# Local attention with the masks cleared on POOL, and zero products at several places of a 16-layer kernel

## The reference

```python
# L3 b: local attention, 16 heads of 8 features, window 128
rel = k_off[None, :] - bs - q_off[:, None]        # bs = 128, keys of three blocks
mask = (abs(rel) <= 128) & valid
scores = where(mask, (q @ k.T) / sqrt(8), -inf)
out = softmax(scores) @ v;  x = x + out @ Wo.T + bo
# L1 a: causal attention with ALiBi slopes, 16 heads of 8 features
# L1 b: LSH attention with 8 hashes
# L2 a: RWKV-6: token shift, five mixtures of x by a narrow product, tanh and
#       a product per kind, then the projections w, r, k, v, g, then a scan
```

## Time and profile before

| | |
|---|---|
| time, three runs | 3257.56 us (median; 3245.51 to 3259.83) |
| the profiled execution | 3265.36 us, span of its records 3263.6 us |
| busy in it | PE 2808.0 us (86%), DVE 1848.9, ACT 1364.3, POOL 766.0 |
| mean granted clock | 0.927 |
| local attention, main stage | from 2946.3 us, the last turned strip's exponentials at 3156.9 |
| RWKV projections, PE's list | from 2258.5 us to 2335 |

### The profile page before, as it was taken

How to read it: one execution, slowest core, us unless ns; L and a number is a source line. 1 busy time by engine, 2 the same in 40 slices (tenths; PEclk the granted TensorE clock), 3 DMA queues, 4 the chain that set the end, 5 groups by cost and what they waited for, 6 DMA issues and landing times. The chain is left out here.

```text
span 3263.6 us, 54321 instructions
## 1 busy us (share of the span) xinstructions
PE 2808.0 (86%) x21112; PEld 1409.7 (43%) x21112; DVE 1848.9 (57%) x3584; ACT 1364.3 (42%) x2665; POOL 766.0 (23%) x725
## 2 busy tenths in 40 slices
PE   6667788999988888899678888898888899888988
PEld 3454375333466333344322222343233444665546
DVE  4424553798762688401588888302495554636744
ACT  3314244533243376632367677422303233234552
POOL 1000063365254200000653240001460001240003
PEclk9788699999999799999779999998899999998999
DMA  3031011222012311000212010000340001022102
GB/s 120 16 102 46 14 43 48 61 70 70 8 49 81 83 26 32 2 1 0 62 30 34 17 19 2 1 1 12 85 134 1 1 1 52 15 78 55 33 13 78
DMA packets 84391, 130.01 MB, mean 40 GB/s; under 512 B 15585, under 2 KB 52929, under 8 KB 82857
## 3 DMA queue, kind: packets, MB, share of 16 engines
q1 hardware_dynamic: 71528, 106.68, 12.0%
q0 software_dynamic: 9152, 16.71, 2.1%
q10 hardware_dynamic: 3456, 3.15, 0.3%
HBM read 99.93 MB, written 25.85 MB: 39 GB/s over the span
## 5 line engine op out<-in xcount | busy, mean ns | idle before, releaser
L1839 DVE TENSOR_REDUCE at_mp<-PS 128x1 f32<-128x384 f32 (+3 forms) x640 | 306.6, 536 | 84.6 <-PE PS L1660 72.4
L1788 ACT ACTIVATE at_pt<-PS 128x384 f32<-128x384 f32 (+3 forms) x704 | 270.3, 455 | 190.0 <-PE PS L1660 156.9
L1652 PE MATMUL PS<-at_kx,at_qx 48*128 48x384 bf16 (+5 forms) x640 | 198.7, 347 | 39.7 <-DVE at_mp L1839 19.8
L113 PE MATMUL PS<-zeros 128*128 128x512 bf16 x834 | 204.0, 389 | 1.2 <-DVE mx_y L1010 1.2
L1680 PE MATMUL PS<-at_qx,at_kx 57*128 57x512 bf16 (+5 forms) x704 | 192.7, 314 | 9.8 <-ACT at_pt L1788 9.4
L4510 DVE CUSTOM_DVE_ANT_0 PS<-PS,ls_pt 128x1024 f32<-128x1024 f32 x128 | 153.9, 1239 | 20.9 <-ACT ls_pt L4363 12.4
L4363 ACT ACTIVATE ls_pt<-PS,ls_far 128x512 f32<-128x512 f32 x256 | 155.3, 686 | 20.9 <-PE PS L4184 16.9
L1660 PE MATMUL PS<-at_above,identb 64*128 64x128 bf16 (+1 forms) x1408 | 161.2, 212 | 0.0
L1660 PE MATMUL PS<-at_other,at_eye 64*128 64x128 bf16 (+1 forms) x1408 | 158.7, 208 | 0.0
L2568 DVE TENSOR_TENSOR_SCAN mb_ring<-PS,mb_ring 128x1024 f32<-128x1024 f32 x64 | 146.6, 2291 | 18.1 <-POOL mb_ring L2501 6.8
L1161 DVE SCALAR_TENSOR_TENSOR X<-PS,small_L,X 128x512 f32<-128x512 f32 x8 | 6.0, 751 | 261.1 <-PE PS L1108 261.1
(11 more groups left out here) (839 smaller groups left out, 6321.7 us busy)
## 6 DMA issues: line engine op xcount, KB each, us to landing
rw_arena<-rw_v_rows SPq DMA_DIRECT2D x32, 512.0 KB, 4.7
dl_arena<-in_fir_bank SPq DMA_DIRECT2D x32, 256.0 KB, 3.2
lnA<-mb_rows SPq DMA_DIRECT2D x16, 512.0 KB, 3.6
XN<-mb_rows SPq DMA_DIRECT2D x16, 512.0 KB, 3.7
ffn_place<-in_ffn_L SPq DMA_DIRECT2D x4, 1152.0 KB, 17.2
x_rows<-mx_t SPq DMA_DIRECT2D x16, 256.0 KB, 2.7
mx_s<-y_rows SPq DMA_DIRECT2D x16, 256.0 KB, 5.0
ffn_place<-in_ffn_L SPq DMA_DIRECT2D x4, 1024.0 KB, 8.1
```

What stands on the lines that cost most here:

```text
L113: k.nc.tensor.matmul(k.PS[:, bank, :], k.zeros16[:, 0:P], k.zeros16[:, :], start=start, stop=start, skip_group_check=True)
L1652: mm = nc.tensor.matmul(PS[:, n % 3, 0:e - c], QX[rows, u % 3, g, blk(i, P)], KX[rows, u % 3, g, c:e], start=True, stop=True)
L1788: nc.scalar.activation(PT[:, y % SLOTS, g, 0:e - c], PS[:, 3 + n % 3, 0:e - c], ACT.Exp, scale=SCALE).then_inc(exp_done, 1)
L1839: nc.vector.tensor_reduce(best, sc, AX.X, ALU.max).then_inc(s_maxed, 1)
```

## The change

In the local attention the turned scores get no masks any more. `cleared` is a new semaphore: once the four exponentials of a strip are there, POOL sets those in the masked triangles to zero (one `affine_select` for each block of `cuts`, over four heads), and the values wait for POOL instead of ACT. `SLOTS` is 4 instead of 3, and the values of a strip are issued two steps after its turned scores instead of one (`LAG`). Ahead of the values of each strip but the first of a half stand two zero products into bank 6; ahead of the maxima of the second half stand four into bank 7. In both attentions `free_misc` comes ahead of the wait for `padded`, three zero products stand in each of the four last steps of the tail, in place of three at the end, and the projections end with 60 instead of 44 (local) and 88 instead of 68 (causal). RWKV: `linger` 12 instead of 6, 14 zero products ahead of the third `narrow`, 3 ahead of the third product of each `mix`. LSH: `linger` 30 instead of 6.

```diff
-    SLOTS = 3
+    SLOTS, LAG = (3, 1) if causal else (4, 2)
...
-                    keep_pe_busy(k, 2, 68 if causal else 44)
+                    keep_pe_busy(k, 2, 88 if causal else 60)
...
-                    if not cuts[x]:
+                    if not (causal and cuts[x]):
                         mm.then_inc(st_ready, 1)
...
                 def values(u, x):
                     h, j, c, e = second[x]
-                    pe.wait_ge(exp_done, N2 * u + HG * x + HG)
+                    if not causal and x != opens[h]:
+                        keep_pe_busy(k, 6, 2, start=False)
+                    if causal:
+                        pe.wait_ge(exp_done, N2 * u + HG * x + HG)
+                    else:
+                        pe.wait_ge(cleared, G2 * u + x + 1)
...
                 def turn_maxima(u, h):
+                    free_misc("m")
+                    if h and not causal:
+                        keep_pe_busy(k, MISC, 4)
                     pe.wait_ge(padded, 2 * u + h + 1)
-                    free_misc("m")
...
+                        if p == UNITS + 1 and x >= 8:
+                            pe.wait_ge(s_maxed, N1 * UNITS)
+                            keep_pe_busy(k, 0, 3)
...
-                        if 1 <= p <= UNITS and 1 <= x <= G2:
-                            values(p - 1, x - 1)
+                        if 1 <= p <= UNITS and LAG <= x < G2 + LAG:
+                            values(p - 1, x - LAG)
...
-                pe.wait_ge(s_maxed, N1 * UNITS)
-                keep_pe_busy(k, 0, 3)
...
-                        if 1 <= p <= UNITS and x == closes[0] + 1:
+                        if 1 <= p <= UNITS and x == closes[0] + LAG:
                             take_output(p - 1, 0)
...
+                def clear(u, x):
+                    h, j, c, e = second[x]
+                    pool.wait_ge(exp_done, N2 * u + HG * x + HG)
+                    for i in cuts[x]:
+                        sign = 1 if i <= j else -1
+                        part = PT[:, (G2 * u + x) % SLOTS, :, i * P - c:(i + 1) * P - c]
+                        ins = pool.affine_select(out=part, in_=part, compare_op=ALU.is_ge, fill=0.0, base=0, pattern=[[0, HG], [sign, P]], channel_multiplier=-sign)
+                    ins.then_inc(cleared, 1)
...
-        layernorm(k, k.X, k.XN, beside=layer_constants)
+        layernorm(k, k.X, k.XN, beside=layer_constants, linger=12)
...
                 def narrow(b):
+                    if b == 2:
+                        keep_pe_busy(k, 6, 14)
...
+                        if i == 2:
+                            if b >= 3:
+                                pe.wait_ge(e_done, b - 2)
+                            keep_pe_busy(k, 6, 3)
...
-            layernorm(k, k.X, k.XN, beside=layer_constants)
+            layernorm(k, k.X, k.XN, beside=layer_constants, linger=30)
```

More of the change, by code:

```diff
@@ L1618, in head_attention @@
         OT, ON, OC = sb("at_ot", [P, 2, BLK]), sb("at_on", [P, BATCH, NT, P]), sb("at_oc", [P, 2, BLK])
-        with stage(nc, "s_ready", "s_maxed", "padded", "m_turned", "own_d", "m_split", "st_ready", "exp_done", "pv_done",
+        with stage(nc, "s_ready", "s_maxed", "padded", "m_turned", "own_d", "m_split", "st_ready", "exp_done", "cleared", "pv_done",
                    "ot_done", "o_turned", "rec_done", "normed", "gathered", "oc_done", "y_ready", "y_added") as (
-                block, s_ready, s_maxed, padded, m_turned, own_d, m_split, st_ready, exp_done, pv_done,
+                block, s_ready, s_maxed, padded, m_turned, own_d, m_split, st_ready, exp_done, cleared, pv_done,
                 ot_done, o_turned, rec_done, normed, gathered, oc_done, y_ready, y_added):
@@ L1686, in turned_masks @@
                     h, j, c, e = second[x]
-                    for i in cuts[x]:
-                        mm = mask(3 + n % 3, i * P - c, 1 if i <= j else 0, head_second(t) // EACH)
-                    if cuts[x]:
+                    if causal and cuts[x]:
+                        for i in cuts[x]:
+                            mm = mask(3 + n % 3, i * P - c, 1, head_second(t) // EACH)
                         mm.then_inc(st_ready, 1)
@@ L1794, in _, with slopes @@
                         take_output(p - 1, 1)
-            if causal:
-                @block.gpsimd
-                def _(pool):
+            @block.gpsimd
+            def _(pool):
+                def slopes():
                     for u in range(1, UNITS):
@@ L1802, in _ @@
                         load_slopes(pool, u)
+                def clear(u, x):
+                    h, j, c, e = second[x]
+                    pool.wait_ge(exp_done, N2 * u + HG * x + HG)
+                    for i in cuts[x]:
+                        sign = 1 if i <= j else -1
+                        part = PT[:, (G2 * u + x) % SLOTS, :, i * P - c:(i + 1) * P - c]
+                        ins = pool.affine_select(out=part, in_=part, compare_op=ALU.is_ge, fill=0.0, base=0, pattern=[[0, HG], [sign, P]], channel_multiplier=-sign)
+                    ins.then_inc(cleared, 1)
+                if causal:
+                    slopes()
+                else:
+                    for u in range(UNITS):
+                        for x in range(G2):
+                            clear(u, x)
             @block.sync
```

## The result

The changed kernel takes 3277.21 us (median of 19 runs, 3261.61 to 3291.29), the kernel before 3259.56 (19 runs, 3245.51 to 3281.86). The ratio is 1.0044, with a 95% interval of 1.0028 to 1.0059: 14.3 us slower (9 to 19; the two medians lie 17.7 apart), less than the 0.5% that the prediction took as its bound. Forecast were 3269 us, a range of 3241 to 3293, and "same" as the likeliest class. The profiled execution took 3278.16 us with a span of 3276.4.

What follows compares the result with a forecast made beforehand. PE was taken to bound the local attention loop, as a chain of score, exponential, fourth score and values at full clock. Loop +30 and repairs -18.5 gave +11.5 us: 3269 us by the median, 3276.9 as profiled; range 3241 to 3293.

Steps and rivals of the forecast that it cites:

- The local loop: Local attention's eight units: added zeros and later values outweigh the removed masks, +3.8 us a unit, +30 us in all.
- the pairs: Two zero products ahead of 8 of 10 products with values: 0.54 us each, 4.3 us a unit, 0.4 hidden.
- the four: Four zero products ahead of the second half's maxima in the local attention: 1.0 us a unit.
- the masks: 112 turned mask products taken off PE in each local attention unit, only partly on the path: -2.3 us a unit.
- The delay: Local attention values two steps later: PE stands 0.8 us for the output copy, about 0.4 at a unit's head.
- The repairs: Added zeros and lingers outside the loop's steps raise the clock: -18.5 us in all, bounds -6 and -30.
- RWKV: RWKV projections: zeros lift the clock, mostly behind the third narrow product; -11 us, bounds -5 and -18.5.
- LSH: Start of the LSH layer: 24 more zeros fill a wait of 6.60 us; -2.5 us, bounds 0 and -3.6.
- The first unit: First unit of the local attention: 16 more zeros in the wait ahead; -1.5 us, bounds 0 and -4.2.
- Masks on the path: Rival, chance 0.22: all local attention masks delay PE (4.5 us a unit), so the change is faster, near 3244 us.
- The clock falls in the loop: Rival, chance 0.17: local attention runs a quarter of its loop at 1.2 GHz, costing 25 us: 3294 us.
- POOL as the bound: Rival, chance 0.09: POOL's clears take 2 us each and bound the local loop: +15 us, near 3284 us.

Runs made afterwards that it cites:

- e5: The changed kernel as it is, run once more: 1.0037 of the kernel before.
- e1: Kernel before plus the RWKV, LSH, attention-projection and tail edits; local attention loop left as before, masks on PE: 0.9948 of the kernel before.
- e12: Kernel before plus the RWKV, LSH, attention-projection and tail edits, local loop as before, run again on another chip: 0.9932 of the kernel before.
- e11: Kernel before with the RWKV edits alone (linger 12, 14 zero products, three in each mixing): 0.9966 of the kernel before.
- e9: Changed kernel without the two zero products ahead of the values, but with the four ahead of the second maxima: 0.9959 of the kernel before.
- e10: Kernel before plus all edits outside the local loop; there masks on PE, no new zeros, values two steps late, four buffers: 0.9946 of the kernel before.
- e2: Changed kernel without the new zero products in the local loop; POOL still clears, values two steps late: 0.9929 of the kernel before.
- e6: Changed kernel with the two zeros ahead of values in the last unit alone and none of the four ahead of maxima: 0.9972 of the kernel before.
- e7: Changed kernel without new zeros in the local loop and with values one step late instead of two, four buffers kept: 0.9975 of the kernel before.

## Why the prediction was right, by its steps

**The sum.** Forecast for an execution like the profiled one: +11.5 us, 3276.9. The profiled execution took 3278.16. This closeness flatters: it holds a clock fall of 10.9 us in the last unit that no term of the sum foresaw, and the terms that follow missed in both directions. By the ratio of all runs it is +14.3 us, against +11.5.

**The local loop, +3.8 us a unit.** Measured +3.44 (27.25 against 23.81). Term by term, from the chain of experiments: the pairs 4.3 forecast, 4.0 measured with what they fill of the wait (4.5 less 0.5; forecast 4.3 less 0.4); the four 1.0 against 0.87; the masks -2.3 against -1.6. Here the reading was right for PE's work (2.2 us less busy) and wrong that all of it shortens the unit. The delay was put at 0.8 + 0.4 and cost 0.2. The stall itself is there (0.72 us ahead of the turning). The 0.4 at the unit's head is not: PE's wait for the exponentials is 0.2 us with and without the delay. Besides, the wait for DVE is 0.2 shorter and PE's busy time 0.3; why is not shown. Two errors of opposite sign, 0.7 and 1.0, nearly cancel. The whole of the stage was forecast at +30 with -3.5 and -1.5 in it, +25, and measured +23.4 where the clock held (`e5`), +35.3 where it fell.

**The repairs, -18.5 us.** Measured alone -17 (`e1`) and -22.5 (`e12`, 0.0068 of 3311), intervals -24 to -10 and -29 to -16. The sum is right, its terms less so.

- RWKV -11 against -11.9 in the trace and -11 by `e11`, but -6 in the profiles of `e1` and `e9`. Its split was off: the stretch to the third narrow product, with the 1.2 us for its 14 zeros, was to give 1.8 - 1.2 = 0.6 us and gave 20.05 - 15.66 = 4.4, since the clock was up from the second narrow product on, where the forecast had it only behind the third. The rest was to give 10.4 and gave 7.5, since the clock still fell to 0.50 from 2286 to 2292 us.
- LSH -2.5, bounds 0 and -3.6. The layer, from its norm to the next, took 179.7 us before and 179.9 in `e11`; in the twelve profiles with the 30 zeros it took 170.8 to 176.3, half of them below 173.9. So -3.4 here and -5.8 as a rule: beyond the bound, which looked at the first 8.1 us alone.
- The tail -3.5 against -3.3: 12.4 us from the last output copy to the next layer norm, now 9.6, and that norm another 0.6 shorter.
- The first unit -1.5. In the changed kernel its first 17.9 us are at 0.53 all the same and its gain can't be told from the zeros' cost. In `e1` and `e12`, from the first score to the second output copy, it takes 42.1 and 42.0 us, before and in `e11` 43.2: -1.2.
- The causal attention 0. Of the 3.1 us by which its loop starts earlier, 1.9 are there at the start of its zero products; `e11`, with the 68 zeros of before, takes 322.7 us for the layer, `e12` with 88 takes 322.7 as well. So 0 stands.
- Not in the sum: the last unit of the local attention, 5.5 and 9.1 us longer in `e1` and `e12` than before, at 0.68 and 0.56.

**The rivals.** Masks on the path: out, `e10` to `e2` gives 1.6 us a unit for them, not 4.5. The clock falls in the loop: in both profiles of the changed kernel not in the units with scores behind the first, but it can in the last one, by 11 us; without the zeros (`e2`, `e6`, `e7`) it falls in units with scores, too, as this rival had it; of the changed kernel's 19 runs the five with a mean clock of 0.941 or 0.942 are the five below 3270 us. POOL as the bound: not at this load; the place from which it decides was given as 1.4 us a clear, the doubled clears of 1.34 us (0.64 each, started 0.70 apart) already cost some 4 us a unit (26.73 against 22.4, at a clock of 0.95). That was without the zeros, in a unit 4.8 us shorter than the one that the forecast spoke of; in that one nobody tried it. A clear was bounded by a row of 1090 ns and took 639.

**The ports.** The forecast left out up to 1.1 us a unit for DVE's small copies beside POOL. In the changed kernel the copy that pads the maxima takes 182 ns, as before, so leaving it out was right. With the clears doubled it takes 379 ns in the mean, the subtraction with both inputs in SBUF (16 x 128) 515 instead of 279, while the reductions out of PSUM stay at 549 and 548. The Trainium skill, "SBUF — State Buffer", section "SBUF: two separate sides", has GpSimd and DVE take turns at a shared pair of ports when the DVE operation is in a two-port mode or has two SBUF inputs. The traces agree for the subtraction and the reductions; that the copy is in such a mode is not shown, only that it is longer. It shows once POOL is two thirds busy, and hardly at one third.

## What to carry to other kernels

A zero product costs its full time (0.22 to 0.24 us here) wherever it stands between the last link of a chain and the product that everyone waits for; put it where PE waits anyway, and price each place by its own wait. Ask first if the clock falls at all where the zeros go: in the loop of before it was at 1.00 without them, and once the masks were gone its falls cost less than the zeros did. Work taken off an engine is not yet time taken off the loop: of 2.2 us of masks 0.6 turned into waiting. And a change that joins a loss and several gains should be run in parts: here 20 us of repairs hid most of a loss of 23 to 35 us.

## What I had not expected

- POOL's select over 128 x 512 fp32 takes 639 ns as 4 blocks of 128 columns in place; another of the same size in this kernel takes 1090.
- The granted clock of one kernel differs between executions: its last unit ran at 1.00 with 25.15 us and at 0.57 with 36.02. The last unit of the kernel before's loop kept 1.00 in both profiles that have it (21.27, 21.26 us), while with the joined changes ahead of it the same loop fell to 0.68 and 0.56 there (26.73, 30.36 us). Why is open: the instructions are the same, only the time at which they come differs.
- A stretch that is nearly the same in all kernels can differ much between executions: the causal attention, from its layer norm to the next, took 319.6 to 332.0 us in the fourteen profiles. A gain of a few us that is read from one pair of profiles needs a second pair, or a run that leaves the edit out.
- A pause of 1.1 us in an otherwise busy loop is followed by a fall in some units and not in others of the same run, and four zero products 8 us ahead of the pause went with none in six units. What links them is not shown.
